# Two attentions on one core: rotations split around the first score, projections a head ahead, operands in two 64-row halves

## What is computed

```python
xn = layernorm(x)
x = x + attn_A(xn) + ffn_B(xn)

# A: causal self-attention, 16 heads of 8 dims, rotary embedding on q and k
qkv = xn @ qkv_w.T + qkv_b ; q, k = rope(q), rope(k)
scores = where(causal, -big, q @ k.T / sqrt(8)) ; out = softmax(scores) @ v ; out @ out_w.T + out_b

# B: a chain of 6 nodes; each is an attention without mask, 8 heads of 16 dims
for c in range(6):
    q, k, v = ew[c] * (nodes[..] @ We[..] + be[..])          # from earlier nodes
    nodes[c] = act_w[c] * mha(q @ Wq, k @ Wk, v @ Wv) @ Wo[c] + q
layernorm(nodes[5]) * ln_g + ln_b
```

## Time and profile before

| | |
|---|---|
| median of 3 runs | 1426.9 us (1423.76 to 1429.07) |
| the profiled execution | 1423.05 us, its span 1421.3 us |
| TensorE busy | 1380.5 us (97%), 26216 matmuls |
| VectorE / ScalarE / GpSimd busy | 1263.0 / 1139.5 / 449.8 us |
| mean granted TensorE clock | 0.991 |

### The profile page before, as it was taken

One profiled execution on the slowest core, in us unless ns is written; L12 is line 12 of the kernel. 1 busy time (PEld: TensorE's weight loads), 2 busy tenths in 40 slices (PEclk: granted clock), 3 DMA queues, 4 the chain that ended last, 5 costly groups with the idle time before them and its releaser, 6 DMA issues.

```text
span 1421.3 us, 60282 instructions
## 1 busy us (share of the span) xinstructions
PE 1380.5 (97%) x26216; PEld 935.3 (66%) x26216; DVE 1263.0 (89%) x1587; ACT 1139.5 (80%) x2133; POOL 449.8 (32%) x936
## 2 busy tenths in 40 slices
PE   6899999999999999999999999999999999999995
PEld 4467777656667666676676766766667666667652
DVE  8889999999989989899899898988989989989895
ACT  3378887688878878888788887887888878878784
POOL 5141115324422433233423332234233432330210
PEclk9899999999999999999999999999999999999998
DMA  8131112343232422333323323233233332321211
GB/s 253 47 116 60 51 59 98 119 142 119 81 127 70 132 97 77 102 109 107 104 78 114 107 74 121 83 123 107 69 101 107 101 107 80 127 98 56 76 38 40
DMA packets 115668, 137.68 MB, mean 97 GB/s; under 512 B 14972, under 2 KB 90109, under 8 KB 115277
## 3 DMA queue, kind: packets, MB, share of 16 engines
q1 hardware_dynamic: 115405, 133.83, 28.7%
HBM read 64.63 MB, written 61.98 MB: 89 GB/s over the span
## 4 chain that ended last, share of the span: by engine, by line
PE 88%; DMA 4%; DVE 3%; SPq 2%; ACT 1%; POOL 1%; issue 1%; ACTq 0%; POOLq 0%; DVEq 0%
PE s L1069 53%; PE cps L1163 26%; PE misc L1069 7%; DMA qs<-mrows 2%; DVE neg_max L971 1%; SPq L431 1%; PE misc L1064 1%; ACT probs L784 1%; DMA dram_raw_b<-csb 1%; PE s L1064 0%; DVE s L967 0%; POOL parts L601 0%; POOL ks L596 0%; POOL full L614 0%; SPq L500 0%
## 5 line engine op out<-in xcount | busy, mean ns | idle before, releaser
L784 ACT ACTIVATE probs<-s 128x512 f32<-128x512 f32 x1792 | 1059.2, 599 | 227.4 <-PE s L1069 166.8
L971 DVE TENSOR_REDUCE neg_max<-s 128x1 f32<-128x1024 f32 x768 | 936.5, 1222 | 62.0 <-PE s L1069 9.1
L1069 PE MATMUL s<-qs,ks 99*32 99x512 bf16 (+2 forms) x7680 | 808.4, 370 | 7.1 <-DMA qs<-mrows 5.1
L1069 PE MATMUL s<-ks,qs 96*32 96x512 bf16 (+2 forms) x7680 | 606.5, 369 | 6.3 <-DMA ks<-dram_qk_a 2.7
L1163 PE MATMUL cps<-probs,vs 128*32 128x256 f32 (+1 forms) x7552 | 591.4, 368 | 0.6 <-ACT probs L784 0.6
L1069 PEld LDWEIGHTS s<-qs,ks 99*32 99x32 bf16 x7680 | 235.8, 94 | 240.6 <-ACT probs L784 96.7
L1163 PEld LDWEIGHTS cps<-probs,vs 128*32 128x32 f32 x7552 | 316.4, 110 | 76.3 <-issue 17.0
L1069 PEld LDWEIGHTS s<-ks,qs 96*32 96x32 bf16 x7680 | 292.5, 97 | 88.6 <-issue 24.5
L633 POOL TENSOR_TENSOR mparts<-neg_max,zeros 128x8 bf16<-128x8 f32 x128 | 26.0, 203 | 796.0 <-DVE neg_max L971 654.3
L967 DVE CUSTOM_DVE_ANT_0 s<-s,mask_q 128x1024 f32<-128x1024 f32 (+7 forms) x256 | 187.8, 785 | 23.5 <-PE s L1069 14.8
L706 POOL TENSOR_TENSOR parts<-full,zeros 128x512 bf16<-128x512 f32 x48 | 61.4, 1280 | 52.2 <-DVE full L949 52.2
(11 more groups left out here) (134 smaller groups left out, 607.6 us busy)
## 6 DMA issues: line engine op xcount, KB each, us to landing
dram_qk_b<-parts SPq DMA_DIRECT2D x48, 384.0 KB, 3.2
qs<-dram_qk_b SPq DMA_DIRECT2D x96, 192.0 KB
ks<-dram_qk_b SPq DMA_DIRECT2D x96, 192.0 KB
dram_qk_b<-parts SPq DMA_DIRECT2D x48, 256.0 KB, 3.2
dram_raw_b<-csb SPq DMA_DIRECT2D x93, 128.0 KB, 4.3
dram_qk_b<-parts SPq DMA_DIRECT2D x48, 128.0 KB, 3.2
vsrc<-srcT SPq DMA_DIRECT2D x12, 512.0 KB, 3.1
ctx_b<-dram_raw_b SPq DMA_DIRECT2D x44, 128.0 KB
```

What stands on the lines that cost most here:

```text
L784: nc.scalar.activation(buf[:, lo:hi], s2[bank][:, 0:hi - lo], ACT.Exp, scale=scale).then_inc(exp_done, 1)
L971: last = ve.tensor_reduce(peak, scores, AX.X, ALU.max, negate=True)
L1069: last = te.matmul(dst[c0:c0 + STRIP, :], lhsT[:, c0:c0 + STRIP], rhs, start=start, stop=stop, tile_position=(0, c0))
```

## The change

1. **Rotations.** `EARLY = 6`: twelve of the sixteen projections (`rot` 0 to 11) are made before the first score; `rot` 12 to 15 stay in units 0 and 1. Two of the six node products (4 and 5) move from before the first score into units 0 and 1, in the bank `misc`; the bias products and the values move to units 2 to 4.
2. **Projections of B's first node, a head ahead.** k and q in AZ go from units 2 to 5 into units 1 to 4, and their cutting and writing from units 3 to 6 into 2 to 5. The load of B's first head is issued at the start of unit 7 of AZ, ahead of the store of the context.
3. **Two halves.** A's heads no longer use `qs`, `ks` but two pairs `qa[k % 2]`, `ka[k % 2]`: heads k and k+2 lie in rows 0 to 50 and 64 to 114 of the same tile (48 rows of data, three of maxima). Scores of A are made with these 48 or 51 rows at row position 0 or 64 of the array; the mask is added with 64 rows at the same row position. The contexts are as before.
4. **Constants.** VectorE sets four `vs` and two `ka` (in the memory of `ctx_b`) instead of twelve rings; GpSimd sets the ones of `ks` in its first microseconds instead of after L593, and makes two more masks.

```diff
+ROWS_A = 6 * DA
+HALF_ROWS = 64
...
-PREP_A_AT = {(2, 2): ("k", 0), (3, 2): ("k", 1), (4, 2): ("q", 0), (5, 2): ("q", 1),
+PREP_A_AT = {(1, 2): ("k", 0), (2, 2): ("k", 1), (3, 2): ("q", 0), (4, 2): ("q", 1),
              (6, 2): ("v", 0), (6, 4): ("v", 1)}
...
-START_AT = {(0, 0): ("bias", 1), (0, 1): ("bias", 2), (0, 2): ("bias", 3),
-            (0, 4): ("rot", 8), (1, 2): ("rot", 9), (1, 4): ("rot", 10), (2, 2): ("rot", 11),
-            (2, 4): ("rot", 12), (3, 2): ("rot", 13), (3, 4): ("rot", 14), (4, 2): ("rot", 15),
-            (4, 4): ("va", 2), (5, 2): ("va", 3)}
+EARLY = 6
+START_AT = {(0, 0): ("prod", 4), (0, 2): ("rot", 12), (0, 4): ("rot", 13), (1, 0): ("prod", 5), (1, 2): ("rot", 14),
+            (1, 4): ("rot", 15), (2, 2): ("bias", 1), (2, 4): ("va", 2), (3, 2): ("bias", 2), (3, 4): ("bias", 3),
+            (4, 2): ("va", 3)}
...
-CUT_AT = {**{k: {} for k in ("A0", "AL", "BE", "T")}, "AZ": {3: [0], 4: [1], 5: [2], 6: [3]},
+CUT_AT = {**{k: {} for k in ("A0", "AL", "BE", "T")}, "AZ": {2: [0], 3: [1], 4: [2], 5: [3]},
...
+        def first_row(which, k):
+            return HALF_ROWS * (k % RING // 2) if which == "A" else 0
+        def operands(which, k):
+            return (qa[k % 2], ka[k % 2]) if which == "A" else (qs[k % RING], ks[k % RING])
...
# SyncE: load_unit, phase
-                if k < UP:
+                if k < UP or kind == "AZ":
                     need(sp, pv_done, added(kind, r, k - RING))
-                else:
+                if k == UP:
                     need(sp, written, 4 * 3 * 16 * PREPS.after(kind, r))
-                for op, dst in ((0, qs[slot]), (1, ks[slot])):
-                    sp.dma_start(dst[0:6 * dims, :],
+                for op, dst in enumerate(operands(which, k)):
+                    sp.dma_start(dst[data_rows(which, k), :],
...
-                    if k < UP - 1 and kind != "T":
+                    if (k < UP - 1 or kind == "AZ") and kind != "T":
                         load_unit(kind, r, k + 1, b)
...
# VectorE, ahead of the first score
             for s in range(RING):
-                for ring in (qs[s][:, :], ks[s][:, :], vs[s][:, :, :]):
-                    ve.memset(ring, 0.0).then_inc(dve_const, 1)
+                ve.memset(vs[s][:, :, :], 0.0).then_inc(dve_const, 1)
+            for n in range(2):
+                ve.memset(ka[n][:, :], 1.0).then_inc(dve_const, 1)
...
+            for n in range(2 * NCH, EARLY):
+                for h in range(2):
+                    turn(2 * n + h, (s2[0], s2[1], cps, misc)[(2 * n + h) % 4])
...
# TensorE
-            def mm_strips(dst, lhsT, rhs, start=True, stop=True):
+            def mm_strips(dst, lhsT, rhs, start=True, stop=True, row=0):
                 for c0 in range(0, 128, STRIP):
                     last = te.matmul(dst[c0:c0 + STRIP, :], lhsT[:, c0:c0 + STRIP], rhs, start=start, stop=stop,
-                                     tile_position=(0, c0))
+                                     tile_position=(row, c0))
+            def mask_strips(dst, row):
+                rows = slice(row, row + HALF_ROWS)
+                for c0 in range(0, 128, STRIP):
+                    here = c0 // HALF_ROWS == row // HALF_ROWS
+                    at, mask = (c0, mask_k) if here else ((c0 + HALF_ROWS) % 128, mask_far[row // HALF_ROWS])
+                    last = te.matmul(dst[c0:c0 + STRIP, :], ident_h[rows, at:at + STRIP], mask[rows, :],
+                                     start=False, stop=True, tile_position=(row, c0))
...
+            for m in range(4 * NCH, 2 * EARLY):
+                pe.wait_ge(xt_sb, m // 4 + 1)
+                pe.wait_ge(rot_done, m - 3)
+                rotate(m, (s2[0], s2[1], cps, misc)[m % 4])
+                if m >= 2 * EARLY - 2:
+                    products(m - 2 * EARLY + 4, half[m - 2 * EARLY + 4])
...
-            pe.wait_ge(rot_done, 4 * NCH)
+            pe.wait_ge(rot_done, 2 * EARLY)
             biases(0)
-            for n in range(2, NODES):
-                products(n)
-            pe.wait_ge(comp_sb, 3 * NODES)
+            pe.wait_ge(comp_sb, 3 * 4)
...
-                    last = mm_strips(bank[:, first - lo:end - lo], ky[0:KALL, t * 128:(t + 1) * 128],
-                                     q[0:KALL, q0 + first - at:q0 + end - at], stop=not diagonal)
+                    last = mm_strips(bank[:, first - lo:end - lo], ky[rows, t * 128:(t + 1) * 128],
+                                     q[rows, q0 + first - at:q0 + end - at], stop=not diagonal, row=row)
                     if diagonal:
-                        last = mm_strips(bank[:, at - lo:at - lo + 128], ident_h[:, :], mask_k[:, :],
-                                         start=False)
+                        last = mask_strips(bank[:, at - lo:at - lo + 128], row)
...
-                                    last = mm_strips(s1[n % 2][:, lo:hi], q[0:KROW, t * 128:(t + 1) * 128],
-                                              ky[0:KROW, lo - at:hi - at])
+                                    last = mm_strips(s1[n % 2][:, lo:hi], q[rows, t * 128:(t + 1) * 128],
+                                                     ky[rows, lo - at:hi - at], row=row)
```

More of the change, by code:

```diff
@@ L273, in dual_attention_kernel @@
         mask_k = sb("mask_k", [128, 128], BF16)
+        mask_far = [sb(f"mask_far{n}", [128, 128], BF16) for n in range(2)]
+        qa = [sb(f"qa{n}", [128, S], BF16) for n in range(2)]
         ones_row = sb("ones_row", [1, 128])
@@ L297, in dual_attention_kernel @@
         exps = {"B": probs, "A": probs + [rec_b]}
+        ka = [ctx_b[:, n * CH:(n + 1) * CH].bitcast(BF16) for n in range(2)]
         s1 = [pb(f"s1_{n}", [128, S]) for n in range(2)]
@@ L514, in phase @@
                             sp.wait_ge(s, 2 * 3 * 16)
-                    if k == UP - 1 and kind not in ("BE", "T"):
+                    if k == UP - 1 and kind not in ("AZ", "BE", "T"):
                         load_unit(kind, r, UP, b)
@@ L572, in _ @@
             pl.memset(power[:, :], -0.5).then_inc(pool_const, 1)
-            pool.wait_ge(pool_const, 5)
+            pool.wait_ge(pool_const, 7)
             pl.tensor_copy(ident_h[:, :], ident[:, :]).then_inc(pool_const, 1)
+            for s in range(RING):
+                pool.wait_ge(pool_const, 8 + s)
+                pl.memset(ks[s][MROW:128, :], 1.0).then_inc(pool_const, 1)
+            pool.wait_ge(pool_const, 8 + RING)
             for n in range(NB):
@@ L661, in phase @@
                                          ).then_inc(x_ready, 1)
-                    if kind == "A0" and 2 <= k < 2 + 2 * NCH:
-                        n = 2 * NCH + k - 2
-                        rest(n)
-                        low_part(n)
+                    if kind == "A0" and k == 0:
+                        for n in range(2 * NCH, EARLY):
+                            rest(n)
+                        for n in range(2 * NCH, EARLY):
+                            low_part(n)
+                    if kind == "A0" and 1 <= k <= 4 * NCH - EARLY:
+                        rest(EARLY + k - 1)
+                        low_part(EARLY + k - 1)
                     if kind == "A0" and k == UP - 1:
@@ L754, in _ @@
             act.wait_ge(wb_in, 16 * 11)
-            products(0)
-            products(1)
+            products(0, half[0])
+            products(1, half[1])
             for g in range(TB // 4):
                 values_a(g)
-            for n in range(2, NODES):
-                products(n)
+            for n in range(2, 4):
+                products(n, half[n])
+            for n in range(2 * NCH, EARLY):
+                high_part(n)
+            for n in range(2 * NCH, EARLY):
+                middle_part(n)
             def phase(kind, r, c, b):
@@ L804, in extra @@
             def extra(kind, r, c, b, ph, what, w):
-                if what == "va":
+                if what == "prod":
+                    products(w, misc)
+                elif what == "va":
                     act.wait_ge(va_ps, w + 1)
@@ L1094, in values_a, with products @@
                 last.then_inc(va_ps, 1)
-            def products(n):
-                need(pe, va_sb, min(n - 1, 2))
-                need(pe, comp_sb, 3 * (n - 3))
+            def products(n, bank):
+                if n < 4:
+                    need(pe, va_sb, min(n - 1, 2))
                 for w in range(3):
-                    last = mm(half[n % 4][:, w * D:(w + 1) * D], we_t_sb[:, (3 * n + w) * D:(3 * n + w + 1) * D],
+                    last = mm(bank[:, w * D:(w + 1) * D], we_t_sb[:, (3 * n + w) * D:(3 * n + w + 1) * D],
                               w4_sb[:, (w * NODES + n) * D:(w * NODES + n + 1) * D])
@@ L1218, in extra @@
                     biases(w)
+                elif what == "prod":
+                    pe.wait_ge(bias_used, 1)
+                    products(w, misc)
                 elif what == "rot":
@@ L1277, in score_piece @@
                 which = kind_at(kind, k, 2)
-                q, ky = qs[(k - 2) % RING], ks[(k - 2) % RING]
```

(5 more changed lines are left out.)

50 lines of the change are left out of this document (31 added, 19 removed).

## The result

The changed kernel takes 1432.4 us in the median of 20 runs (1420.7 to 1437.9), the kernel before 1426.1 us beside it (1422.3 to 1430.1): ratio 1.003, interval 1.0015 to 1.0044. The forecast was 1428 in a range of 1406 to 1446. Two things hide behind this small number. A's dense units became faster, not slower, and the granted clock of TensorE became worse in stretches that were not the same in every execution. The mean granted clock (the share of TensorE's full speed that it was allowed, over a whole execution) is 0.987 to 0.992 for the executions of the kernel before; for the changed kernel's 20 it is 0.973 to 0.987, and its times follow it: 1420.7 to 1424.0 us at 0.986 and 0.987, 1437.0 to 1437.9 at 0.973 to 0.976. The profiled execution is one of the former: 1422.8 us, span 1421.0.

A forecast was written before the change was run, and what follows sets the result against it. TensorE was taken to bound A, VectorE B. Terms -1.1 - 0.4 - 4.0 + 5.6 - 0.5 + 1.7 = +1.3 us gave 1424.4 against the profiled execution, 1428 against the median; range 1406 to 1446.

The forecast's parts named there:

- It is wrong if the AL unit is none of these: Sign in A's dense units: context copies 6.70 us apart as forecast, 6.05 to 6.1 if switches free, 7.5 without overlap.
- The switches: A's units: ten layout switches between contexts and scores at 0.10 us each, 1.0 us a unit; bounds 0 and 0.10 each.
- The rival of a cheap switch: A's units: a switch is cheap or free where only rows change, VectorE's 6.05 us decides; 1407 us, chance 0.27.
- The overlap: A's units: s1 and s2 matmuls in opposite row halves run together, saving 0.80 us of 6.50; bounds 0 and 0.80.
- order is kept, so an instruction starts when its half is free and its predecessor has started: Rule for TensorE's two row halves in A's turns, from which 0.80 us of overlap a unit was counted.
- s2's first piece (512) runs alone: Each A turn: nothing overlaps s2's first 512 columns; only its mask then runs beside s1's first piece.
- The rival without overlap: A's dense units: the halves don't run at once, the switches remain, +23.7 us in all; 1451 us, chance 0.18.
- Units 0 to 2: A's start: rotations, products and values moved, -0.4 us, between -2 and +2; low clock lasting into unit 1, +1.6.
- B0's entry: B0's units 0 and 1: 18 switches a unit, no overlap; +1.7 us, between 0 and 3.6.
- The rotations: Units 3 to 7: rotations 13 to 15 and one value set leave, two small bias products come; -4.0 us.
- The first score: Start: GpSimd's and VectorE's memsets leave the chain; score not before about 36.5, -1.1 us, between 0 and -1.5.
- Part 2: A's last unit: B's loads ahead of the store, row of maxima 0.3 us earlier; -0.5 us, 0 to -1.8.

The follow-up runs named there:

- one half alone: Changed kernel with every A head in the lower row half, so nothing can overlap: 1466.6 and 1469.0 us, ratio 1.028 against the kernel before.
- the added work: Changed kernel plus ten unused strip sets of 128 rows in units 0 and 1 of A0: 1429.2 us, ratio 1.0023 against the kernel before.
- either end old: Changed kernel with only heads 0 and 1, or only 30 and 31, in the old 96- and 99-row layout: 1425.3 us (0.9987), 1424.3 us (0.9979).
- both ends old: Changed kernel with heads 0, 1, 30 and 31 in the old 96- and 99-row layout: 1420.7 us, ratio 0.9957 against the kernel before.

## Why the prediction was right, and where not

The time lies in the range, 4.4 us above the forecast, and the change is the small loss that was forecast. That it came so near is luck. The dense units came out 8.7 us better than forecast, and a low clock for which the sum had almost nothing took that back and more. By the prediction's own sign ("It is wrong if the AL unit is none of these": 6.70, 6.05 to 6.1, 7.5) its account of A's dense units was wrong: the unit is 6.31.

**The switches** were right. In AL each way costs 0.10 us beyond the work, as at 136.96 to 137.11 and 137.57 to 137.72; 0.10 was taken from rows where the columns change, and a change of rows alone costs the same. The Trainium skill, "TensorEngine Tiling (Array Packing)", section Key Properties, says that a change of mode drains the engine; the trace agrees, with 0.10 us for it. The rival of a cheap switch (AL unit 6.05) fell.

**The overlap** was mis-sized: 0.80 a unit was forecast, 6.50 + 0.96 - 6.31 = 1.15 came, even with TensorE idle for 0.25 us a unit (51.40 - 49.38 in eight units), as in the wait for ScalarE of 0.19 at 136.24. The failed step is "order is kept, so an instruction starts when its half is free and its predecessor has started", with its conclusion "s2's first piece (512) runs alone". `s1`'s first piece starts 0.03 us after it and passes the waiting mask, though the program has the order piece, mask, `s1`. So "TensorE executes in the order of the program", above, doesn't hold for opposite halves. That made the AL unit 6.31 instead of 6.70, 8.7 us over 23 units. The rival without overlap (7.5) was measured with one half alone, 7.61, and fell too. The Trainium skill, "TensorE: Matmul & The Clock Gate", Part 3, says that matmuls start in program order; here 136.27 before 136.46 speaks against it for opposite halves, and the measurement decides.

**Units 0 to 2** failed: -0.4 (-2 to +2, +1.6 if the low clock lasts) against +6.2. With parts 1 and 2 alone it is +0.9, inside the bounds; the other 5.3 came with the halves. The prediction saw that a longer low clock was possible, but tied it to the rotations moved out of the way, priced only unit 1, and never asked what the halves do to it. The step that failed is this term: a low clock worth +1.6 at most. For B0's entry it priced switches alone (+1.7, measured +2.6, inside 0 to 3.6), where a low stretch costs 5.7 us (a first unit of 15.94, with the added work) to 14.3 when it comes. That this second place lifts the median from the profiled 1422.8 to 1432.4 is inferred: its one trace is of an execution at 1422.8 us, but its median clock, 0.980 against 0.987, means some 20 us more at the low level, and the experiments with either end old point there.

**The rotations** were right: -4.2 in units 3 to 7 with parts 1 and 2 alone, -4.0 forecast. **The first score** came at 36.32, just before the 36.5 held possible. With before's constants it comes at 37.59 and 37.36 in two traces, so most of this gain is part 4's. **Part 2** was forecast at -0.5 and can't be told from scatter: with parts 1 and 2 and no halves unit 31 takes 8.36, and in other kernels without halves there 8.06 and 7.92, the wait behind it 1.68, 1.39 and 1.26. With halves and without part 2 unit 31 is 9.58 and the wait 2.28, so it may be worth more there; each of these is one execution.

That leaves the profiled execution 1.6 us under the forecast made against it (1424.4), and the median 4.4 above its own. Not settled: what B's unchanged turns add between two executions (2.3 us here), and the weight of rows against switches.

## What to carry to other kernels

Packing two small contractions into two row halves does pay in a dense stretch, if the two streams are independent: count the overlap by half, not by program order, and a change of tile rows at 0.10 us. The dense units gained 0.19 us of 6.50 here, after the switches. Then look where the same matmuls run among waits, at the start and where one stage hands over to the next: there fewer rows in each matmul can cost more in granted clock than the packing gains, and padding with zero rows may be the faster layout. Read the mean clock of every run before a median is explained by one profile, and before contexts are grouped to save switches, see who lives on the scores between them.

## What the runs showed of the hardware that was not expected

- A matmul for one row half starts ahead of one that stands before it in the program and waits for the other half: 136.27 against 136.46.
- 96 rows cut to 66, the rest zeros, and nothing else changed: mean granted clock from 0.992 to 0.994 down to 0.985 to 0.988 (0.991 in one of ten), with a stretch of 27.2 us at 0.50 in the trace.
- The low level stays through stretches in which TensorE is busy throughout (17.00 of 17.00 us, 33.90 of 33.90, by the modelled ends). The Trainium skill, "TensorE: Matmul & The Clock Gate", Part 1, puts the low level down to an idle TensorE and lets it end once TensorE is busy. The fall at B0's entry does come after waits of 1.43 to 2.28 us; how long it lasts, and the fall in unit 2 with both ends old (busy for 4.87 of the 5.00 us before), don't fit.
- Ten more strip sets of 128 rows in units 0 and 1 took the low stretch from 27.2 to 3.3 us, in the one trace there is.
